# One step less between the exponentials and the weighing of the values, and one buffer less for each of its three tiles

## The reference

```python
q = (Q @ w_q.T).reshape(B, S, G, HG, HD)      # 8 groups of 4 heads of 8 elements
k = (K @ w_k.T).reshape(B, S, G, HD)
v = (V @ w_v.T).reshape(B, S, G, HD)
scores = jnp.einsum('bnghd,bmgd->bnghm', q, k) / jnp.sqrt(jnp.float32(HD))
scores = jnp.where(causal, scores, NEG_INF)
attn = jax.nn.softmax(scores, axis=-1)
out = jnp.einsum('bnghm,bmgd->bnghd', attn, v).reshape(B, S, D)
return out @ w_o.T + b_o
```

## Time and profile before

| | us |
|---|---|
| median of three executions | 1522.51 |
| the three | 1521.06, 1522.51, 1524.45 |
| the profiled execution | 1524.45 |
| its span, first to last instruction | 1522.5 |
| mean granted TensorE clock | 0.951 of full |
| PE busy, DVE busy, ACT busy, POOL busy in the span | 1356.1, 1160.4, 983.8, 819.3 |
| second attention, first raw score to last logits read | about 1130 to 1389 |

### The profile page before, as it was taken

How to read it: one execution, slowest core, us unless ns; L and a number is a source line. 1 busy time by engine, 2 the same in 40 slices (tenths; PEclk the granted TensorE clock), 3 DMA queues, 4 the chain that set the end, 5 groups by cost and what they waited for, 6 DMA issues and landing times. The chain is left out here.

```text
span 1522.5 us, 29404 instructions
## 1 busy us (share of the span) xinstructions
PE 1356.1 (89%) x11216; PEld 1148.6 (75%) x11216; DVE 1160.4 (76%) x2303; ACT 983.8 (65%) x2168; POOL 819.3 (54%) x865
## 2 busy tenths in 40 slices
PE   0677999999999999999999996999948999995995
PEld 0566999999999999999999985677613555554994
DVE  8799888888888888888898897633345787864564
ACT  4796878777887778777877775312114665562773
POOL 5776666656566675566664453101104776673672
PEclk9799999999999999999999998999966999995997
DMA  3101100100000000001001001351065202004553
GB/s 105 56 8 28 33 4 16 36 15 15 22 15 16 22 16 24 13 15 36 14 5 51 2 2 34 114 61 38 28 109 68 34 15 57 16 15 138 201 208 132
DMA packets 63547, 69.99 MB, mean 46 GB/s; under 512 B 6736, under 2 KB 56112, under 8 KB 63280
## 3 DMA queue, kind: packets, MB, share of 16 engines
q1 hardware_dynamic: 60800, 60.74, 15.6%
q0 software_dynamic: 2432, 7.34, 1.4%
q10 hardware_dynamic: 176, 0.04, 0.0%
HBM read 55.56 MB, written 12.34 MB: 45 GB/s over the span
## 5 line engine op out<-in xcount | busy, mean ns | idle before, releaser
L880 POOL TENSOR_TENSOR RB<-YS,M 128x512 bf16<-128x512 f32 x128 | 161.5, 1262 | 247.5 <-DVE YS L739 247.5
L566 ACT ACTIVATE QT<-B,sm 128x256 f32<-128x256 f32 x256 | 131.1, 564 | 164.3 <-PE B L423 164.3
L443 PE MATMUL SS<-QT,KT 128*128 128x256 f32 x512 | 156.0, 399 | 12.2 <-DVE mx L694 12.1
L876 POOL TENSOR_TENSOR yy<-vv,half 128x12 f32<-128x12 f32 x64 | 148.4, 2318 | 5.3
L391 PE MATMUL PA<-WH,XQ 128*128 128x256 f32 x512 | 139.6, 305 | 5.4 <-ACT SQ L595 5.4
L393 PE MATMUL PA<-WL,XQ 128*128 128x256 f32 x512 | 128.7, 285 | 0.0
L713 DVE TENSOR_TENSOR QN<-QN,yy 128x512 f32<-128x512 f32 x128 | 125.6, 981 | 3.1 <-POOL yy L876 3.1
L706 DVE TENSOR_REDUCE vv<-SQ 128x6 f32<-128x768 f32 x128 | 120.6, 942 | 0.0
L1639 ACT ACTIVATE P<-PO,mcf 128x1024 f32<-128x1024 f32 x64 | 71.4, 1116 | 75.6 <-PE PO L1518 75.6
L694 DVE TENSOR_REDUCE mx<-SS 128x4 bf16<-128x512 f32 x128 | 88.0, 688 | 42.0 <-PE SS L435 41.3
L1799 POOL TENSOR_SCALAR_AFFINE_SELECT P<-P 128x1024 f32<-128x1024 f32 x64 | 70.3, 1099 | 91.6 <-ACT P L1639 91.2
(11 more groups left out here) (339 smaller groups left out, 4389.7 us busy)
## 6 DMA issues: line engine op xcount, KB each, us to landing
W<-in_w SPq DMA_DIRECT2D x16, 1024.0 KB
Q<-qsc SPq DMA_DIRECT2D x48, 128.0 KB
WR<-in_wprojT SPq DMA_DIRECT2D x16, 256.0 KB, 3.0
K<-ksc SPq DMA_DIRECT2D x12, 256.0 KB
qsc<-T POOLq DMA_DIRECT2D x8, 384.0 KB, 4.2
X<-in_x SPq DMA_DIRECT2D x4, 512.0 KB, 6.1
CR<-in_xctxT SPq DMA_DIRECT2D x8, 256.0 KB, 2.8
RSM<-rsm_d SPq DMA_DIRECT2D x16, 128.0 KB, 4.4
```

The lines of the kernel that those rows point to most:

```text
L443: pe.matmul(SS[:, 256 * z:256 * z + 256], k[:, 128 * z:128 * z + 128], q[:, 256 * z:256 * z + 256], start=True, stop=False)
L566: a.activation(QT[i % 2][:, o:o + 256], B1[:, o:o + 256], ACT.Identity, bias=col(n + "b"), scale=col(n + "w"))
L876: p.tensor_tensor(yy[j % 2][:], v_, half[:], ALU.pow).then_inc(s_rstd, 1)
L880: p.tensor_tensor(RB[i % 2][:], YS[:], M[:], ALU.subtract).then_inc(s_rb, 1)
```

## The change

Everything in the second attention from the evacuation and the weighing on stands one step sooner: weigh at distance 10 instead of 11, and with it the evacuation, turn, normalising, output turn, output projection, residual, next turn, logits, the preparation of the values and the bias, and the numbers in `NEXT`. The loops have one step less (82 instead of 83). The distances of raw, maximum, shifted, exponential, select, upper and both lowers stay. P1 has 3 buffers instead of 4, PH1 and PL1 have 2 instead of 3, with the waits on `s_LO` counted to match. Two waits that keep the PSUM tile SS safe are rewritten.

```diff
-        PH1 = [sb(f"PE1{i}", [128, 2, 256], FR) for i in range(3)]
-        PL1 = [sb(f"PL1{i}", [128, 2, 256], FR) for i in range(3)]
-        P1 = [sb(f"P1{i}", [128, 1024]) for i in range(4)]
+        PH1 = [sb(f"PE1{i}", [128, 2, 256], FR) for i in range(2)]
+        PL1 = [sb(f"PL1{i}", [128, 2, 256], FR) for i in range(2)]
+        P1 = [sb(f"P1{i}", [128, 1024]) for i in range(3)]
...
-        NEXT = {32: 0, 48: 1, 64: 2, 76: 3, 80: 4}
+        NEXT = {31: 0, 47: 1, 63: 2, 75: 3, 79: 4}
...
             if b >= 3:
-                pe.wait_ge(s_y0, N + 2 * b - 5)
+                pe.wait_ge(s_oe, b - 2)
             pe.matmul(SS[0:32, 256:384], mxb[b % 2][:], negib[:], start=True, stop=True).then_inc(s_mt, 1)
...
             pe.wait_ge(s_y0, N + 2 * b + 2)
-            pe.wait_ge(s_mte, min(b + 4, NB))
...
-            for n in range(N1 + 19):
+            for n in range(N1 + 18):
...
-                if 0 <= n - 11 < N1:
-                    pe_weigh_1(pe, n - 11)
-                b = every(n, 4, 37, NB - 4)
+                if 0 <= n - 10 < N1:
+                    pe_weigh_1(pe, n - 10)
+                b = every(n, 4, 36, NB - 4)
                 if b is not None:
                     pe_logits(pe, b)
+                b = every(n, 4, 16, NB)
+                if b is not None:
+                    pe_out_turn(pe, b)
                 b = every(n, 4, 17, NB)
                 if b is not None:
-                    pe_out_turn(pe, b)
-                b = every(n, 4, 18, NB)
-                if b is not None:
                     pe_out_proj(pe, b)
-                b = every(n, 4, 35, NB - 4)
+                b = every(n, 4, 34, NB - 4)
                 if b is not None:
                     pe_next_turn(pe, b)
-                u = every(n, 2, 14, 2 * NB)
+                u = every(n, 2, 13, 2 * NB)
                 if u is not None:
                     pe_turn_1(pe, u)
...
             a.wait_ge(s_ST, N + i + 1)
-            if i >= 4:
-                a.wait_ge(s_LO, N + i - 3)
+            if i >= 3:
+                a.wait_ge(s_LO, N + i - 2)
...
             a.wait_ge(s_sel, i + 1)
-            if i >= 3:
-                a.wait_ge(s_LO, N + i - 2)
+            if i >= 2:
+                a.wait_ge(s_LO, N + i - 1)
```

More of the change, by code:

```diff
@@ L1530, in pe_weigh_1 @@
             e = g0 // 2
-            pe.matmul(OT[u % 2][:], VE[b % 2][:, e, :], PH1[i % 3][:], start=i % 2 == 0, stop=False)
-            pe.matmul(OT[u % 2][:], VE[b % 2][:, e, :], PL1[i % 3][:], start=False, stop=False)
-            pe.matmul(OT[u % 2][:], VO[b % 2][:, e, :], parity(P1[i % 4], 1), start=False, stop=i % 2 == 1).then_inc(s_LO, 1)
+            pe.matmul(OT[u % 2][:], VE[b % 2][:, e, :], PH1[i % 2][:], start=i % 2 == 0, stop=False)
+            pe.matmul(OT[u % 2][:], VE[b % 2][:, e, :], PL1[i % 2][:], start=False, stop=False)
+            pe.matmul(OT[u % 2][:], VO[b % 2][:, e, :], parity(P1[i % 3], 1), start=False, stop=i % 2 == 1).then_inc(s_LO, 1)
         def pe_turn_1(pe, u):
@@ L1636, in act_expo_1 @@
             a.wait_ge(s_ST, N + i + 1)
-            if i >= 4:
-                a.wait_ge(s_LO, N + i - 3)
-            a.activation(P1[i % 4][:], STB, ACT.Exp, bias=mcf[:, b:b + 1], scale=SC1).then_inc(s_ex, 1)
+            if i >= 3:
+                a.wait_ge(s_LO, N + i - 2)
+            a.activation(P1[i % 3][:], STB, ACT.Exp, bias=mcf[:, b:b + 1], scale=SC1).then_inc(s_ex, 1)
         def act_upper(a, i):
             a.wait_ge(s_sel, i + 1)
-            if i >= 3:
-                a.wait_ge(s_LO, N + i - 2)
-            a.activation(PH1[i % 3][:], parity(P1[i % 4], 0), ACT.Copy).then_inc(s_up1, 1)
+            if i >= 2:
+                a.wait_ge(s_LO, N + i - 1)
+            a.activation(PH1[i % 2][:], parity(P1[i % 3], 0), ACT.Copy).then_inc(s_up1, 1)
         def act_evac_out(a, u):
@@ L1665, in act_attention_1 @@
             after_feed_forward_0(a)
-            for n in range(N1 + 19):
-                b = every(n, 4, 18, NB)
+            for n in range(N1 + 18):
+                b = every(n, 4, 17, NB)
                 if b is not None:
                     act_out_turn(a, b)
-                b = every(n, 4, 36, NB - 4)
+                b = every(n, 4, 35, NB - 4)
                 if b is not None:
@@ L1679, in act_attention_1 @@
                     act_upper(a, n - 9)
-                u = every(n, 2, 13, 2 * NB)
+                u = every(n, 2, 12, 2 * NB)
                 if u is not None:
@@ L1697, in dve_lower @@
             v.wait_ge(s_up1, i + 1)
-            v.tensor_tensor(PL1[i % 3][:, 0, :], P1[i % 4][:, 0:256], PH1[i % 3][:, 0, :], ALU.subtract).then_inc(s_lo1, 1)
+            v.tensor_tensor(PL1[i % 2][:, 0, :], P1[i % 3][:, 0:256], PH1[i % 2][:, 0, :], ALU.subtract).then_inc(s_lo1, 1)
         def dve_normalise(v, u):
@@ L1756, in dve_attention_1 @@
                     dve_lower(v, n - 10)
-                u = every(n, 2, 15, 2 * NB)
+                u = every(n, 2, 14, 2 * NB)
                 if u is not None:
                     dve_normalise(v, u)
-                b = every(n, 4, 38, NB - 4)
+                b = every(n, 4, 37, NB - 4)
                 if b is not None:
                     dve_logits(v, b)
-                b = every(n, 4, 19, NB)
+                b = every(n, 4, 18, NB)
                 if b is not None:
@@ L1797, in pool_select @@
             p.wait_ge(s_ex, N + i + 1)
-            p1 = P1[i % 4][:].rearrange("p (h n) -> p h n", n=128)
+            p1 = P1[i % 3][:].rearrange("p (h n) -> p h n", n=128)
             p.affine_select(out=p1, in_=p1, compare_op=ALU.is_ge, fill=0.0, base=0, pattern=[[0, 8], [1, 128]],
@@ L1803, in pool_lower @@
             p.wait_ge(s_up1, i + 1)
-            p.tensor_tensor(PL1[i % 3][:, 1, :], P1[i % 4][:, 512:768], PH1[i % 3][:, 1, :], ALU.subtract).then_inc(s_lo2, 1)
+            p.tensor_tensor(PL1[i % 2][:, 1, :], P1[i % 3][:, 512:768], PH1[i % 2][:, 1, :], ALU.subtract).then_inc(s_lo2, 1)
         def pool_next_root(p, k):
@@ L1830, in pool_attention_1 @@
                     pool_lower(p, n - 9)
-                b = every(n, 4, 7, NB)
+                b = every(n, 4, 6, NB)
                 if b is not None:
                     pool_values(p, b)
-                b = every(n, 4, 8, NB)
+                b = every(n, 4, 7, NB)
                 if b is not None:
```

## The result

| | before | after |
|---|---|---|
| median, both kernels on the same chips in turn, 14 executions each | 1518.86 us | 1531.71 us |
| ratio, 95% interval | | 1.008 (1.0056 to 1.0103) |
| span of the profiled execution | 1522.5 us | 1527.4 us |
| first raw load (L1490) to the last weighing's load (L1531) | 238.1 us | 247.6 us |
| first raw load to the last logits read | 259.0 us | 268.5 us |

The account below looks back on a forecast made before the run. PE was taken to set the pace in steady steps, DVE around its work for the next stage. Terms 1.2 + 1.1 + 4.2 + 2.0 + 0.4 + 0.6 = 9.5 us on the 1522.51 median gave 1532.0 us, range 1528 to 1537.

Parts of the forecast that it names:

- head: Start of the second attention, steps 10 to 13: one added weighing delays the following steps, +1.2 us, range 0.4 to 1.8.
- scaling: Batches from steps 33 and 49, where DVE sets the pace: +0.2 us each, +0.4 in all; length hardly changes.
- constants and the batch behind: Steps 37 to 41: 0, since routing constants hold DVE and POOL whatever PE does; steps 41 to 45: +0.5 us.
- steady batches: Four-step batches of steps 17 to 33: each grows from 12.55 to 13.60 us, +1.05, together +4.2 us.
- The rule: Weighing of step n, W(n), starts no sooner than 3.66 us behind the shifted of the step before, S(n - 1).
- The bound that DVE's remainder might be the last to end: If DVE's remainder ended last, a steady batch would wait 0.1 us instead of 1.05: sum 3, time 1525.5 us.
- The recurrence: Step-by-step sums of weighing starts in a steady batch: waits of 0.70 and 0.35 us, gaps about 3.9, 3.3, 3.0, 3.3.
- The sign set for it: Idle time before L1531's loads becomes 10 to 15 us, with POOL's remainder or the mask as releaser.
- Drain: Steps 64 to the last weighing: waits for remainders cost +0.6 us; fewer weighings behind the last shifted give back 0.1.
- A: Rival: the remainders come in time, so +3 us or less, no change that can be told from none; chance 0.17.
- B: Rival: faster, every remainder is there, the drain saves about 1.9 us and the clock rises earlier: 1518.5 us; chance 0.07.
- C: Rival: short waits cost PE its clock, 1.6 us in seven of fifteen batches, 11 more: 1543 us; chance 0.08.

## Why the prediction was right

The forecast was 1532.0 us with a sum of 9.5 us. The medians differ by 12.9 us, and the interval of the ratio asks for 8.5 to 15.6 us. That the absolute number was met within 0.3 us (1531.71) is luck: the kernel before had a median 3.6 us lower in this comparison (1518.86) than in the three executions from which the forecast started (1522.51). In the profile, from the first raw load to the last weighing, 9.5 us are there. Term by term:

| Steps | forecast | measured |
|---|---|---|
| first raw to 13 (head) | +1.2 | +0.3 (41.66 to 41.93) |
| 13 to 17 | +1.1 | +1.2 |
| 17 to 33 | +4.2 | +4.3 |
| 33 to 37 and 49 to 53 (scaling) | +0.4 | -0.4 |
| 37 to 45 (constants and the batch behind) | +0.5 | +1.2 |
| 45 to 49, 53 to 61 | +1.5 | +1.7 |
| 61 to the last weighing | +0.6 | +1.2 |

The terms of the steady batches were right. That the sum fits to 0.1 us is luck again: the head and the scaling came 1.7 us lower than forecast, the constants, the drain and the rest 1.7 us higher.

- **The rule** W(n) >= S(n - 1) + 3.66, read from one step of the trace of before, was met by 3.69 in the trace after, and its slope held when the chain was shortened (12.7 us a batch expected, 12.83 measured) and lengthened (14.84 and 14.88). The bound that DVE's remainder might be the last to end falls.
- **The recurrence** gave gaps of 3.90, 3.33, 3.04 and 3.33; they are 3.90, 3.37, 3.04 and 3.37. The mechanism and its size are shown. One sentence ahead of it miscounts: it calls two of the four gaps shorter than 3.33, but its own rows have three (2.63, 3.20, 2.82). The recurrence does not rest on it; it has two waits a batch, and two came. The sign set for it came too. This row of the wait list over the whole stage (1125 to 1390) has no counterpart before the change:

```profile
PE B L1531 <- POOL PL L1803: 13.8, 25, 1.3
```

  Not all of it is loss, since PE's waits for the maxima shrank (in the same list from 17.0 to 12.1 us).
- **The head** was the worst term for its size. The first weighing did start late, 1.27 behind its shifted:

```profile
1155.76 0.13 PEld L1518 LDWEIGHTS PO<-Q,K 49*128 49x128 bf16 x4 [0.20 <-issue]
...
1156.03 0.89 POOL L1803 TENSOR_TENSOR PL<-P,PE 128x256 fp32r<-128x256 f32 x1
...
1157.03 0.29 PEld L1531 LDWEIGHTS B<-PE,VE 128*128 128x128 f32 x1 [1.15 <-issue]
...
1160.73 0.11 PEld L1518 LDWEIGHTS PO<-Q,K 49*128 49x128 bf16 x4
```

  But the clock rose in time for step 11's shifted (a load of 0.11, 3.70 behind the weighing instead of 4.25), and most of the forecast delay did not come. In the run with the old buffers it rose nearly 6 us later and the head took 44.4. So this term depends on the execution by 2.5 us, more than the 1.4 us of its range, and 0.3 is luck.
- **Scaling.** Forecast 0.2 more for each of the two batches, measured 0.35 and 0.07 less. The sign of this small term was wrong; which wait became shorter was not taken apart.
- **The constants.** I had 0 for steps 37 to 41, since constants hold everything there, and 0.5 for the batch behind. They cover nothing: over both the loss is 1.2, about the same as over two batches without them (13.69 against 13.15 each), and it is 1.1 with the constants gone. That the first batch grew by 2.3 and the second shrank by 1.1 is in the main the low clock behind the stall (about 1.6 us), which in the earlier trace rows lay from 1264.0 to 1278.8 and now lies one batch earlier (0.88 from 1253.0 to 1267.0).
- **Drain.** Twice the forecast, against the one trace of the old order in which the clock stayed up behind the late residual; against the other, with the constants early (37.0), the same stretch would come out 0.3 us shorter than before. PE's waits for the remainders come to about 4 us there, and only a part of them overlaps the 2.5 us that the late residual had held it up before. The following rows show the two waits ahead of the last weighing, which answers to the earlier trace rows:

```profile
1367.02 0.11 PEld L1518 LDWEIGHTS PO<-Q,K 49*128 49x128 bf16 x4 [0.17 <-issue]
...
1368.64 0.19 PEld L1531 LDWEIGHTS B<-PE,VE 128*128 128x128 f32 x1 [1.51 <-DVE PL L1697]
...
1370.93 0.19 PEld L1531 LDWEIGHTS B<-PE,VE 128*128 128x128 f32 x1 [0.51 <-issue]
...
1372.87 0.19 PEld L1531 LDWEIGHTS B<-PE,VE 128*128 128x128 f32 x1
```

  The last one stands 5.85 behind its shifted, against 5.64 before: where the prediction gives back 0.1 us, 0.2 more are taken.
- **Buffers, turn of the maxima, dropped wait**: 0 forecast; 205.4 without them and 205.7 with them.
- **Rivals.** A and B are out: no gap of 2.63 is left in the batches. C is out for this change: the granted clock is 1.00 from 1180.0 to 1234.7 with PE busy 50.72 of 54.70 us, so waits of 0.7 us did not lower it in this kernel. With the longer chain it stayed at 1.00 too, over four batches with PE busy 50.72 of 58.94 us. As a mechanism C exists in this kernel: with the small buffers in the old order, where PE was busy 12.97 of 15.62 us, the clock fell in steady batches. The rule of the Trainium skill that I weighed (TensorE: Matmul & The Clock Gate, A second HAM failure mode: psum-queue depth-cycling, on small idle times between groups of matmuls) does not show in the steady batches of the changed kernel.

## What to carry to other kernels

In a hand-written software pipeline, write down for each operation the earliest start its inputs allow behind a fixed point of the step before, and compare it with the shortest gap between steps, not with the mean: here 3.33 us was needed, the mean was 3.14 before, and three gaps in four were shorter. A step taken out of a pipeline saves little when the stages ahead of it set the number of steps, and it costs in every step whose slack it takes. Buffers and distances are to be changed together: the same three buffers less are free at distance 10 and cost 2.8% at distance 11.

## What was unexpected

- The rise of PE's clock at the head came 34.7 us behind the first raw load in the changed kernel's profile and 40.5 us in that of the same order with the old buffers, with the same list of work on PE (38.6 before the change). This alone moves the stage by 2.5 us, as much as a change that one would want to judge, and it is why stretches that begin behind it are the better measure.
- After the change the 0.7 us waits in every batch left the clock at 1.00. A stall of 2.7 us ahead of step 41 before the change was followed by a stretch at 0.88. The stall of 2.5 us in the drain was not in that execution, and in the one with the constants early the same stall was. So one stall has two prices here, 1.5 us apart, and a stretch of some 200 us carries this scatter.
- An operation that is hidden in the steady steps (0.6 us on POOL, in the old order) cost 12 us in the steps where another engine had already used up the slack, 5.9 of them because PE's clock fell. A steady cycle that does not change is no proof that a longer operation is free.
